# Ten of the gather windows move into the second layer: five destination blocks of layer 1 are summed from gathered rows instead of from streamed blocks

## The chip, the cores and the metric

The kernel runs on one core of one Trainium2 chip. The metric is the device time of one execution in microseconds (us). Three executions of the kernel before took 1515.6, 1515.96 and 1516.13 us; their median is 1515.96 us.

## The reference: a three-layer mean-aggregating graph network

There are 6,250 nodes with 128 features and 206,250 directed edges (100,000 random pairs in both directions and one loop for each node), sorted by destination. What is computed, cut to its core:

```python
def _mean_agg(x, src, dst, n):
    msg_sum = jax.ops.segment_sum(x[src], dst, num_segments=n)
    cnt = jax.ops.segment_sum(jnp.ones((src.shape[0], 1), x.dtype), dst, num_segments=n)
    return msg_sum / jnp.maximum(cnt, 1.0)
def _sage_conv(x, src, dst, Wl, bl, Wr):
    return _mean_agg(x, src, dst, x.shape[0]) @ Wl.T + bl + x @ Wr.T

h = jnp.maximum(_layernorm(x), 0.0)
h = relu(batch_norm(sage_conv(h, ..., Wl0, bl0, Wr0)))   # 128 -> 256 features
h = relu(batch_norm(sage_conv(h, ..., Wl1, bl1, Wr1)))   # 256 -> 256
h = sage_conv(h, ..., Wl2, bl2, Wr2)                     # 256 -> 128
out = x + log_softmax(h)
```

## The kernel before

The 6,250 destination nodes are cut into 25 blocks of 250 (`BD`), the source nodes into 49 tiles of 128 (`NA`). The segment sum is done as a dense product. In layer 0 the kernel builds, for each destination block, a matrix of edge counts (49 tiles of 128 x 250, f16, 3 MB in all), uses it at once and stores it in DRAM as `c_blocks`. Layers 1 and 2 load these blocks back into `ring`, which has two slots, and multiply them with the features. The features are kept in f16 as a high and a low part (`parts`, seen as `wide` in layer 1 with 256 features and as `small` in layer 2 with 128).

**Sweeps.** In layers 1 and 2 the blocks are visited in a fixed order (`orders`). Two blocks that lie in the two slots are swept together (`sweeps`, lines 158 to 162): one matmul of 500 columns serves both. A layer-1 pair sweep has 49 tiles x 2 parts (high, low) x 2 halves of the features = 196 such matmuls. What is left over is swept alone with matmuls of 250 columns. In layer 1, 25 blocks make 12 pair sweeps and one single sweep. Sweep 0 of a layer is special: TensorE also transposes the normalized features (`pe_pair`), ScalarE rounds them to the high part (`act_hi`) and VectorE subtracts to get the low part (`dve_lo`), 25 pairs of tiles in turn. A count called a step runs through the later sweeps (`places`, line 170): one step is two matmuls of 500 columns in a pair sweep, or four of 250 in a single one, and there are 49 of them for each block.

**The rest of a block.** After a sweep VectorE scales the sums to means (`dve_means`), and TensorE computes the two linear products of the block, 16 f32 matmuls in layer 1 (`pe_product1`, L1165 and L1168). They are put into the next sweep at given steps (`dense_lin`, line 179): at step `NA // 4` = 12 and 49 steps later.

**Gathered blocks.** Some blocks (`loose`) are not swept. Their features come row by row from a table in DRAM: `table_store` writes the f16 features there (high and low part side by side, 512 B a row in layer 2, 1024 B in layer 1), and GpSimd fetches 128 rows with one indirect DMA (`pool_round`). TensorE adds them up with a one-hot matrix (`pe_round`, L1193): the 125 nodes of half a block, a window, lie in four groups of 31 or 32 nodes, and a round takes one tile of 128 edges for each of them, so it has 4 indirect DMAs and 4 matmuls whose outputs go to 32 partitions each; the ninth and last round of a window has 5. Three rounds' buffers (`NGOT`) let GpSimd run ahead; a later round first waits for `t_round`, that TensorE has used the buffer. The steps at which TensorE takes the rounds are spread evenly over the layer (`at`, line 198). After a window TensorE transposes its sums (`pe_group_turn`), and ScalarE scales them (`act_gmean`). Before the change the gathered blocks are 21 and 22, and only in layer 2: 4 windows, 36 rounds, 148 DMAs. Layer 1 gathers nothing.

**Queues.** All order is written out by hand, one stream for each engine. SyncE issues the block loads (`block_load`, L1552: quarters of a block, each when the quarter of the slot has been used), GpSimd the indirect DMAs.

## Time and profile before

| | |
|---|---|
| median of three executions | 1515.96 us |
| the profiled execution | 1516.13 us, of it 1514.4 us span |
| TensorE busy | 1408.8 us (93%) |
| VectorE, ScalarE, GpSimd busy | 545.7, 531.9 and 282.5 us |
| mean granted TensorE clock | 0.987 |

The span runs from the first to the last instruction. A granted clock of 1.00 is 2.4 GHz. The stages follow one another: layer 0 to about 560 us, sweep 0 of layer 1 to 621 us, the rest of layer 1 to 1187 us, layer 2 to the end. In a timeline row the first number is the start, the second the time from the first start to the last end of a run of equal instructions; a run's matmuls overlap, so what one costs is the distance of two starts divided by their number.

### The profile page before, as it was taken

How to read it: one execution, taken by the hardware profiler on the slowest of the kernel's cores; microseconds unless marked ns; L12 is line 12 of the kernel's file. 1: busy time of each engine (PE TensorE's matmuls, PEld its weight loads, DVE VectorE, ACT ScalarE, POOL GpSimd, SP SyncE). 2: the span in 40 equal slices, each digit the busy share in tenths (PEclk: the TensorE clock that was granted, in tenths of full speed). 3: DMA queues.
4: the chain of work that ended last, by engine and by line, in shares of the span. 5: the costliest groups of instructions: out<-in, count | busy, mean ns of one | idle time of the engine just before them, and what ended most of it. 6: DMA issues, size and time to landing. Idle time of an engine off the chain costs nothing.

```text
span 1514.4 us, 31217 instructions
## 1 busy us (share of the span) xinstructions
PE 1408.8 (93%) x13761; PEld 873.5 (58%) x13761; DVE 545.7 (36%) x1001; ACT 531.9 (35%) x866; POOL 282.5 (19%) x266
## 2 busy tenths in 40 slices
PE   1399999999999999999999999999999899999996
PEld 1377777777767775554545545454557764444444
DVE  6968777777778753100000000000001212222123
ACT  4887878787877847200000000000000420000001
POOL 3422131313040200000000000000000024666640
PEclk9999999999999999999999999999999999999998
DMA  5244444544444442333443333434321487888882
GB/s 161 91 186 155 160 168 189 189 181 181 175 162 175 176 154 82 133 132 127 140 161 132 133 122 133 142 132 157 130 92 47 126 308 269 316 313 308 315 303 80
DMA packets 73812, 258.78 MB, mean 171 GB/s; under 512 B 12544, under 2 KB 42296, under 8 KB 70456
## 3 DMA queue, kind: packets, MB, share of 16 engines
q1 hardware_dynamic: 62860, 238.64, 44.3%
q0 software_dynamic: 7600, 16.45, 3.6%
q8 instruction: 112, 1.84, 0.5%
q10 hardware_dynamic: 3212, 1.63, 0.4%
q14 instruction: 28, 0.23, 0.0%
HBM read 171.85 MB, written 84.83 MB: 169 GB/s over the span
## 4 chain that ended last, share of the span: by engine, by line
PE 84%; ACT 7%; DVE 2%; issue 2%; another core or an unknown queue 2%; DMA 1%; POOL 0%; ACTq 0%; DVEq 0%; SPq 0%
PE bank L1568 30%; PE cells L1568 16%; PE bank L1150 15%; PE cells L1142 7%; PE bank L1165 4%; PE bank L1168 4%; ACT ring L653 3%; PE bank L1571 2%; ACT junk L601 2%; PE bank L1910 1%; PE cells L1649 1%; DMA parts<-in_pairs_dram,last_i 1%; PE cells L1193 1%; PE cells L1638 0%
## 5 line engine op out<-in xcount | busy, mean ns | idle before, releaser
L1568 PE MATMUL bank<-ring,parts 128*128 128x500 f16 x2254 | 501.6, 375 | 0.6 <-DVE parts L1623 0.4
L653 ACT CAST ring<-cells 128x980 f16<-128x980 f32 (+1 forms) x325 | 335.4, 1057 | 109.6 <-PE cells L1142 96.5
L1568 PEld LDWEIGHTS bank<-ring,parts 128*128 128x128 f16 x2254 | 214.2, 96 | 246.4 <-issue 7.1
L1150 PE MATMUL bank<-ring,parts 128*128 128x250 f16 (+1 forms) x2450 | 319.7, 272 | 2.7 <-ACT ring L653 2.3
L517 POOL DMA_INDIRECT hots<-table,src_i x148 | 140.3, 948 | 792.7 <-DMA table<-parts 708.6
L1568 PE MATMUL cells<-ring,parts 128*128 128x500 f16 x1176 | 251.3, 372 | 0.0
L881 DVE TENSOR_TENSOR hots<-iotas,tab 128x980 f16<-128x980 f16 (+3 forms) x262 | 245.6, 996 | 11.3 <-ACT tab L617 11.3
L1150 PEld LDWEIGHTS bank<-ring,parts 128*128 128x128 f16 (+1 forms) x2450 | 216.3, 98 | 35.2 <-ACT ring L653 3.7
L1695 ACT ACTIVATE Z<-bank,vec 128x250 f32<-128x250 f32 x48 | 19.9, 465 | 530.2 <-PE bank L1168 530.2
L1568 PEld LDWEIGHTS cells<-ring,parts 128*128 128x128 f16 x1176 | 112.5, 96 | 134.8
L961 DVE BATCH_NORM_STATS2 st<-Z 128x6 f32<-128x250 f32 x96 | 35.5, 412 | 394.5 <-ACT Z L1695 361.6
L1142 PE MATMUL cells<-hots 64*128 64x49 f16 x4670 | 107.2, 186 | 43.7 <-DVE hots L881 34.8
L1142 PEld LDWEIGHTS cells<-hots 64*128 64x128 f16 x4670 | 80.4, 95 | 96.9 <-issue 51.5
L1822 ACT ACTIVATE junk<-rows_i 128x128 f32<-128x128 f32 (+1 forms) x49 | 14.7, 301 | 231.1 <-DVE rows_i L1874 160.9
L881 DVE TENSOR_TENSOR parts<-iotas,tab 128x2560 f16<-128x2560 f16 (+1 forms) x88 | 83.0, 984 | 1.2 <-ACT tab L617 1.2
L1168 PE MATMUL bank<-agm,wl 128*128 128x250 f32 x288 | 76.5, 374 | 0.0
L1165 PE MATMUL bank<-Z,wr 128*128 128x250 f32 x288 | 76.4, 374 | 0.0
L469 POOL DMA_INDIRECT rows_i<-in_dst_rows_dram,row_i x25 | 36.3, 1451 | 198.1 <-DVE row_i L746 192.3
L1168 PEld LDWEIGHTS bank<-agm,wl 128*128 128x128 f32 x288 | 54.8, 190 | 6.0
L1165 PEld LDWEIGHTS bank<-Z,wr 128*128 128x128 f32 x288 | 52.4, 189 | 7.5
L1601 ACT ACTIVATE Z<-Z,bnw 128x256 f32<-128x256 f32 (+2 forms) x76 | 45.9, 655 | 1.8 <-DVE bnw L1590 1.6
L1142 PE MATMUL cells<-parts 64*128 64x49 f16 x1580 | 35.7, 186 | 11.1 <-ACT ring L653 8.5
(198 smaller groups left out, 771.5 us busy)
## 6 DMA issues: line engine op xcount, KB each, us to landing
ring<-c_blocks SPq DMA_DIRECT2D x132, 750.0 KB
c_blocks<-ring SPq DMA_DIRECT2D x25, 3062.5 KB
ring<-c_blocks SPq DMA_DIRECT2D x44, 812.5 KB
rcb<-rc_row SPq DMA_DIRECT2D x73, 125.0 KB
Z<-in_x_dram SPq DMA_DIRECT2D x4, 768.0 KB, 7.2
out_dram<-rows_i SPq DMA_DIRECT2D x24, 128.0 KB
hots<-table,src_i POOLq DMA_INDIRECT x148
table<-parts SPq DMA_DIRECT2D x2, 768.0 KB
```

The source lines that it names most:

```text
L469: pool.indirect_dma_start(out=rows_i[:, k, :], out_offset=None, in_=dst_rows, in_offset=bass.IndirectOffsetOnAxis(ap=row_i[:, c:c + 1], ax ...
L517: pool.indirect_dma_start(out=got[layer][:, 5 * (r % NGOT) + i, :], out_offset=None, in_=tables[layer], in_offset=bass.IndirectOffsetOnAxi ...
L601: act.activation(junk[:, 0:R], smp_i[:, :], ACT.Sign, bias=thr_h[:, c:c + 1], scale=-1.0, accum_out=s1[:, c:c + 1]).then_inc(a_sample, 1)
L653: act.copy(blk[c % 2][:, :, :].rearrange("p a (d g) -> p a d g", d=GD)[:, :, :, GPS * i:GPS * i + n], cells[t % 2][:, :, 0:n * NA].rearran ...
L881: ins = dve.tensor_tensor(o[:, 0:q, :, :], iota2[:, 0:w, :].unsqueeze(1).to_broadcast((P, q, w, 2)), place.unsqueeze(2).to_broadcast((P, q ...
L961: dve.bn_stats(st[:, m, b, :], Z[:, m, BD * b:BD * b + BD]).then_inc(v_stats, 1)
L1142: ins = pe.matmul(cells[t % 2][:, h, NA * g:NA * g + NA], bs[HE * h:HE * h + HE, q0 + g // 2, :, g % 2], ps[HE * h:HE * h + HE, q0 + g // ...
L1150: return pe.matmul(bank[b][:, 0:BD], view[0:r, a, part, m * P:m * P + P], blk[s][0:r, a, :], start=(a, part) == (0, 0), stop=(a, part) == ...
L1165: pe.matmul(bank[b][:, BD * m:BD * m + BD], wr[layer][:, k, m * P:m * P + P], Z[:, k, BD * c:BD * c + BD], start=(k == 0), stop=False)
L1168: ins = pe.matmul(bank[b][:, BD * m:BD * m + BD], wl[layer][:, k, m * P:m * P + P], mean[:, k, :], start=False, stop=(k == nk - 1))
L1568: ins = pe.matmul(bank[b][:, 0:2 * BD].rearrange("p (s d) -> p s d", s=2), lhs, ring[0:r, :, BD * a:BD * a + BD], start=(a, part) == (0, 0 ...
L1601: act.activation(Z[:, k, c0:c0 + w], Z[:, k, c0:c0 + w], ACT.Relu, bias=bnw[:, layer, 5, k:k + 1], scale=bnw[:, layer, 4, k:k + 1]).then_i ...
```

## The change

`NGB` (2 gathered blocks) becomes `NG1` = 5 for layer 1 and `NG2` = 2 for layer 2. The loose blocks are now 18 to 22: layer 1 gathers all five, layer 2 blocks 18 and 19. Layer 1 then visits 20 blocks, which make 10 sweeps in the layer's loop after sweep 0: 8 pair sweeps and 2 single ones (before 11 pair sweeps and 1 single). SyncE and ScalarE write the layer-1 table during sweep 0. The layer-1 products move from step 12 to step 6 of a sweep. The tables of windows grow from 16 to 40 rows, and the total of the loose counts is summed from two parts.

```diff
--- before.py
+++ after.py
@@ -24,7 +24,8 @@
 NHOT = 4
 NBT = 4
 NTAB = 8
-NGB = 2
+NG1 = 5
+NG2 = 2
 WIN = 31
 WT = (9, 9, 9, 10)
 WE = 1280
@@ -54,7 +55,7 @@
     NB = N // BD
     NT = -(-E // P)
     FULL = NA - 1
-    assert N % BD == 0 and GPS * NA <= 512 and NT * P <= EP and NB >= NGB + 4
+    assert N % BD == 0 and GPS * NA <= 512 and NT * P <= EP and NB >= NG1 + 4
     flat_pairs = pairs.rearrange("r c two -> (r c) two")
     pe, dve, act, pool, sp = nc.tensor, nc.vector, nc.scalar, nc.gpsimd, nc.sync
 
@@ -115,8 +116,8 @@
         return NST * (h // NHB) + min(NST, SPH * (h % NHB) + SPH) - 1
 
 
-    loose = list(range(NB - 2 - NGB, NB - 2))
-    gathered = [[], [], loose]
+    loose = list(range(NB - 2 - NG1, NB - 2))
+    gathered = [[], loose, loose[0:NG2]]
     W = 8 * len(loose)
     wins = [[2 * loose.index(b) + h for b in gathered[layer] for h in range(2)] for layer in range(3)]
     gbase = [0, 0, len(wins[1])]
@@ -177,7 +178,7 @@
 
 
     dense_lin = [{}, {}, {}]
-    for layer, a0 in ((1, NA // 4), (2, NA // 4)):
+    for layer, a0 in ((1, NA // 8), (2, NA // 4)):
         o = orders[layer]
         for u, js in enumerate(sweeps[layer][1:]):
             for k, j in enumerate(sweeps[layer][u]):
@@ -1090,9 +1091,15 @@
                                           ALU.add).then_inc(v_own, 1)
                         own.up()
                         parts_at = [batches[q][0] + 1 for q in range(len(batches)) if loose_part(q)]
-                        assert len(parts_at) == 1
                         dve.tensor_scalar(tot[:, NB + 1:NB + 2], tot[:, parts_at[0]:parts_at[0] + 1], -1.0, None,
-                                          ALU.mult).then_inc(v_tot, 1)
+                                          ALU.mult).then_inc(v_own, 1)
+                        dve.wait_ge(v_own, own.up())
+                        for k in parts_at[1:-1]:
+                            dve.tensor_tensor(tot[:, NB + 1:NB + 2], tot[:, NB + 1:NB + 2], tot[:, k:k + 1],
+                                              ALU.subtract).then_inc(v_own, 1)
+                            dve.wait_ge(v_own, own.up())
+                        dve.tensor_tensor(tot[:, NB + 1:NB + 2], tot[:, NB + 1:NB + 2],
+                                          tot[:, parts_at[-1]:parts_at[-1] + 1], ALU.subtract).then_inc(v_tot, 1)
                         dve_norms(own)
                     elif c == NB and i == 7:
                         dve_spread(own)
@@ -1663,6 +1670,9 @@
             v = vbase[1]
             rcb_load(v)
             rcb_load(v + 1)
+            for k in range(2):
+                table_here(sp, a_hi1, v_lo1, 2, xcuts[k + 1])
+                table_store(sp, 1, wide, xcuts[k], xcuts[k + 1])
             for u in range(1, len(sweeps[1])):
                 for k in range(4):
                     for j in sweeps[1][u]:
@@ -1688,6 +1698,11 @@
                     act_normalize(0, 2, t + 2, a_relu1)
                 if t + 1 < npair:
                     act_hi(wide, 2, 256, t + 1, t_pair, a_hi1)
+                if t == (xcuts[3] - 1) // 2 + 2:
+                    table_here(act, a_hi1, v_lo1, 2, xcuts[3])
+                    table_store(act, 1, wide, xcuts[2], xcuts[3])
+            table_here(act, a_hi1, v_lo1, 2, NA)
+            table_store(act, 1, wide, xcuts[3], NA)
             for t in range(NA * (D1 - 2)):
                 for b in products(1, t - 2):
                     act.wait_ge(t_lin, lin_no(1, b))
```

TensorE at the start of layer 1's sweep 1, as written before (L1568 is the sweep, L1165 and L1168 the product):

```order
L1568 MATMUL bank<-ring,parts 128x500 x12
L1568 MATMUL cells<-ring,parts 128x500 x26
L1165 MATMUL bank<-Z,wr 128x250 x2
L1168 MATMUL bank<-agm,wl 128x250 x2
L1165 MATMUL bank<-Z,wr 128x250 x2
L1168 MATMUL bank<-agm,wl 128x250 x2
L1568 MATMUL cells<-ring,parts 128x500 x98
```

The same place now (L1575 is the sweep, L1172 and L1175 the product, L1200 a gather round, whose outputs are 32 partitions x 512 columns):

```order
L1575 MATMUL cells<-ring,parts 128x500 x14
L1172 MATMUL bank<-Z,wr 128x250 x2
L1175 MATMUL bank<-agm,wl 128x250 x2
L1172 MATMUL bank<-Z,wr 128x250 x2
L1175 MATMUL bank<-agm,wl 128x250 x2
L1575 MATMUL cells<-ring,parts 128x500 x62
L1200 MATMUL cells<-hots,tab 32x512 x4
L1575 MATMUL cells<-ring,parts 128x500 x22
L1200 MATMUL cells<-hots,tab 32x512 x4
```

The product stands 12 matmuls earlier (6 steps), and from step 37 on a round stands after every 20 to 22 sweep matmuls, fewer where a product lies between.

GpSimd in layers 1 and 2, before:

```order
L1966 COMPARE_AND_BRANCH
L517 DMA hots<-table,src_i 128x256 x148
L1966 UNCONDITIONAL_BRANCH
```

and now:

```order
L1981 COMPARE_AND_BRANCH
L518 DMA hots<-table,src_i 128x512 x370
L518 DMA hots<-table,src_i 128x256 x148
L1981 UNCONDITIONAL_BRANCH
```

370 indirect DMAs of 128 rows x 512 numbers (1024 B) have come in ahead of the 148 of layer 2.

## Rows read from the trace of the kernel before

**Rows 1.** The page: TensorE's busy line, the chain by engine, two DMA queues

```profile
PE 1408.8 (93%) x13761; PEld 873.5 (58%) x13761; DVE 545.7 (36%) x1001; ACT 531.9 (35%) x866; POOL 282.5 (19%) x266
PE 84%; ACT 7%; DVE 2%; issue 2%; another core or an unknown queue 2%; DMA 1%; POOL 0%; ACTq 0%; DVEq 0%; SPq 0%
...
q1 hardware_dynamic: 62860, 238.64, 44.3%
q0 software_dynamic: 7600, 16.45, 3.6%
```

**Rows 2.** Busy time by stage (stretch: length, busy us of each engine, clock, DMA)

```profile
core 0: us, PE busy (x) PEld busy (x) DVE busy (x) ACT busy (x) POOL busy (x), PEclk, DMA share, GB/s
...
621.05:1150.67 529.62, 529.62 (x2511) 272.95 (x2509) 34.28 (x88) 18.23 (x44) 0.00 (x0) 1.00 0.39 132
...
1232.60:1514.40 281.80, 262.26 (x1379) 130.94 (x1377) 62.34 (x159) 25.41 (x132) 140.28 (x148) 0.96 0.79 276
```

**Rows 3.** Timeline of TensorE, one pair sweep of layer 1 with its two products

```profile
677.91 20.86 PE L1568 MATMUL bank<-ring,parts 128*128 128x500 f16 x98
698.60 1.00 PE L1165 MATMUL bank<-Z,wr 128*128 128x250 f32 x4
...
701.98 15.37 PE L1568 MATMUL bank<-ring,parts 128*128 128x500 f16 x72
717.19 1.01 PE L1568 MATMUL cells<-ring,parts 128*128 128x500 f16 x4
```

**Rows 4.** Timeline of TensorE, the single sweep and layer 1's end

```profile
1167.97 10.43 PE L1571 MATMUL bank<-ring,parts 128*128 128x250 f16 x96
1178.24 1.01 PE L1212 MATMUL bank<-Z,wr 128*128 128x250 f32 x4
```

**Rows 5.** Timeline of TensorE, two gather rounds and a turn in layer 2

```profile
1412.14 0.29 PE L1193 MATMUL cells<-hots,tab 128*32 128x256 f16 x4
1412.37 3.13 PE L1568 MATMUL bank<-ring,parts 106*128 106x500 f16 x14
...
1417.75 0.40 PE L1193 MATMUL cells<-hots,tab 128*32 128x256 f16 x5
1418.09 3.76 PE L1568 MATMUL bank<-ring,parts 128*128 128x500 f16 x17
...
1423.81 0.27 PE L1202 MATMUL cells<-cf,gsum 128*128 128x128 f32 x1
1424.01 0.29 PE L1193 MATMUL cells<-hots 128*32 128x256 f16 x4
```

**Rows 6.** Timeline, last table stores and first gathers of layer 2 (512 B rows)

```profile
1231.16 1.43 ACTq L458 DMA_DIRECT2D table<-parts  x2
1232.59 1.57 SPq L1552 DMA_DIRECT2D ring<-c_blocks  x2
1237.22 1.06 POOL L517 DMA_INDIRECT hots<-table,src_i  x1 [708.65 <-DMA table<-parts]
...
1238.59 0.96 POOL L517 DMA_INDIRECT hots<-table,src_i  x1 [0.30 <-issue]
1239.86 0.95 POOL L517 DMA_INDIRECT hots<-table,src_i  x1 [0.30 <-issue]
```

**Rows 7.** Timeline of GpSimd, indirect DMAs of 1024 B rows in layer 0

```profile
16.10 0.94 POOL L469 DMA_INDIRECT rows_i<-in_dst_rows_dram,row_i  x1 [0.30 <-issue]
17.35 0.94 POOL L469 DMA_INDIRECT rows_i<-in_dst_rows_dram,row_i  x1 [0.30 <-issue]
...
90.40 2.00 POOL L469 DMA_INDIRECT rows_i<-in_dst_rows_dram,row_i  x1 [15.37 <-DVE row_i L746]
```

**Rows 8.** The line L469, all 25: from issue to landing

```profile
DMA to landing us min/median/max: 2.7/3.5/6.1
```

**Rows 9.** Groups of GpSimd by line: mean ns of one

```profile
L517 POOL DMA_INDIRECT hots<-table,src_i x148 | 140.3, 948 | 792.7 <-DMA table<-parts 708.6 <-issue 42.2 <-remote 23.5
L469 POOL DMA_INDIRECT rows_i<-in_dst_rows_dram,row_i x25 | 36.3, 1451 | 198.1 <-DVE row_i L746 192.3 <-issue 5.8
```

**Rows 10.** Timeline, the end of sweep 0 of layer 1

```profile
618.96 0.42 DVE L1623 TENSOR_TENSOR parts<-cells,parts 106x256 f16<-106x256 f32 x1 [1.00 <-ACT parts L1617]
...
621.09 1.64 DVE L890 SCALAR_TENSOR_TENSOR agm<-bank,bnw,rcb 128x250 f32<-128x250 f32 x4 [1.71 <-PE bank L1568]
```

**Rows 11.** Timeline of SyncE's queue around the start of layer 1

```profile
545.97 4.81 SPq L450 DMA_DIRECT2D rcg<-rc_row  x4
560.62 0.82 SPq L407 DMA_DIRECT2D rcb<-rc_row  x2
582.17 40.20 SPq L1552 DMA_DIRECT2D ring<-c_blocks  x8
```

**Rows 12.** Timeline of TensorE, layer 2, after a wait

```profile
1258.55 0.40 PE L1193 MATMUL cells<-hots,tab 128*32 128x256 f16 x4 [3.17 <-DVE tab L1009]
1258.88 5.18 PE L1568 MATMUL bank<-ring,parts 128*128 128x500 f16 x12
1263.85 1.32 PE L1910 MATMUL bank<-Z,wr 128*128 128x250 f32 x4
```

## Prediction, made before the changed kernel ran

> **What bounds the kernel now.** I read the page first. TensorE is busy 1408.8 of 1514.4 us, and 84% of the chain that ended last lies on it [rows 1]. Then the table by stage: between 621.05 and 1150.67 us, layer 1 after its first sweep, TensorE is busy for the whole 529.62 us at a granted clock of 1.00, GpSimd does nothing, VectorE 34 us, ScalarE 18 us, and the DMA engines are used to 0.39 [rows 2]. So there TensorE alone sets the pace, and one us less of matmuls is one us less of time, as long as nothing that is added becomes slower than TensorE. Last I read the timeline of one sweep, for what a matmul costs from start to start: 98 matmuls of 500 columns take 698.60 - 677.91 = 20.69 us, 0.211 each; a product takes 701.98 - 698.60 = 3.38 us [rows 3]; a matmul of 250 columns (1178.24 - 1167.97) / 96 = 0.107 us [rows 4].
>
> **What goes from TensorE.** Three pair sweeps fewer: 3 x 196 x 0.211 = 124.1 us. One single sweep more: 196 x 0.107 = 21.0 us. Net -103.1 us. The 25 products stay 25; those of the gathered blocks only move.
>
> **What comes to TensorE.** Ten windows of nine rounds: 80 rounds of 4 matmuls and 10 of 5. Layer 2 shows the operation with 256 columns: the next sweep matmul starts 0.23 us after a round of 4 and 0.34 us after one of 5 [rows 5]. Four matmuls one after the other would take 4 x 0.107 = 0.43 us, so the four run side by side, and only the fifth, which goes to the same 32 outputs as the fourth, adds a stream of 0.11. With 512 columns a stream is 0.213 us (0.211 x 512 / 500 is 0.216; both read off the same row). From below: only the stream doubles, a round of 4 costs 0.23 + 0.107 = 0.34, one of 5 0.34 + 2 x 0.107 = 0.55, together 80 x 0.34 + 10 x 0.55 = 32.7 us. From above: everything doubles, 0.46 and 0.68, together 43.6 us. Ten turns of two transposes: one costs 0.20 with what surrounds it [rows 5], I take 0.3, 3 us. TensorE's own sum is -103.1 + 32.7 + 3 = -67.4 us, or -56.5 by the upper price.
>
> The excess of a round over its stream, 0.12 us, could be a fixed price or grow with the columns. The Trainium skill (TensorEngine Tiling (Array Packing), Key Properties) says that going to another tiling mode drains the engine, which here happens twice a round and does not depend on the columns. By that rule the lower price holds (-67.4); by plain scaling the upper one does. The trace agrees that there is an excess, 0.23 against a stream of 0.107, and has only one width, so it can't say which.
>
> **GpSimd, the new second bound.** 80 x 4 + 10 x 5 = 370 indirect DMAs come into layer 1, where GpSimd has been idle. One takes 0.95 us and the next starts 0.30 us later: a pitch of 1.25 us, in layer 2 with 512 B rows [rows 6] and in a quiet piece of layer 0 with 1024 B rows [rows 7] (17.35 - 16.10). So the size of a row doesn't matter, and GpSimd needs 370 x 1.25 = 462 us. When can it start? The last piece of the table is ready when VectorE ends the last low part at 618.96 + 0.42 = 619.4 [rows 10]. In layer 2 GpSimd started 1237.22 - 1231.16 = 6.1 us after the last stores were issued, of half as many bytes and with a block load beside them [rows 6]; for twice the bytes I take 6 to 10, so GpSimd starts at 626 to 630. TensorE reaches the first round at step 37: 621.05 + 37 x 0.422 + 3.38 = 640.1. By then the first round's 4 DMAs are issued (635 at the latest) and, with 2.5 to 3.5 us to land [rows 8], there.
>
> From the first round on both walk at nearly the same pace. TensorE: round 89 stands at step 840, so 803 steps x 0.422 = 338.9, 18 products of swept blocks and 4 of gathered ones 22 x 3.38 = 74.4, rounds 32 (43 by the upper price), turns 3: 448 us (459). GpSimd: three rounds are fetched ahead, the other 87 have 358 DMAs x 1.25 = 447.5 us, and the last needs 2.5 us more to land: 450. By the lower price GpSimd is late by about 2 us, and since the rounds with 5 DMAs (6.25 us) meet a TensorE pace of 448 / 89 = 5.0 us with about 7 us of lead, I take 5 us of waits of TensorE for rows; by the upper price none. So the two bounds give -62.4 and -56.5. I take the middle, -60: 1516.1 - 60 = 1456 us. The profiled execution (1516.13, with 1.7 us outside its span) stands 0.2 us above the median.
>
> **What costs nothing, and its cover.** (a) Five 3 MB blocks fewer are loaded, but the DMA share was 0.39 and loads were issued three quarters of a sweep ahead: no gain. (b) The gathers bring 370 x 131 KB = 48.5 MB. Queue 0 moved 16.45 MB in 3.6% of 1514 us, 302 GB/s when it had the engines [rows 1]: 161 us over 470, which raises the DMA share from 0.39 to about 0.73. Layer 2 ran at 0.79 [rows 2] and TensorE was busy 262 of 282 us there, so this cover is thin; it is a rival below. (c) SyncE's two table stores stand ahead of the first block loads. The first load moves from 582.17 [rows 11] to when half of the low parts exist, about 592; that data is needed at 621, and 3 MB with a store beside it need about 10 us at 300 GB/s. Covered by 18 us. (d) ScalarE issues three stores (0.4 and 1.43 us, [rows 6]) in sweep 0, where it waits for TensorE in every turn: under 1 us. (e) The product at step 6 begins 2.5 us after the sweep; the means it needs end at 621.09 + 1.64 = 622.7 [rows 10], TensorE is there at 623.6. (f) The count columns `rcg` are 2.5 times as many short pieces: 4.81 us of issue become some 12, from 545.97 to 558, before SyncE's next work at 560.62 [rows 11]. (g) VectorE's one more subtraction, two wider casts, ten one-hots and twenty foldings lie on an engine that is busy for 34 of 530 us. (h) Layer 2 keeps 36 rounds and 148 DMAs, for other blocks.
>
> **Rivals.** *Rows that come late.* GpSimd's pitch or the landing is what TensorE waits for, because 1024 B gathers share the DMA engines with block loads. With a lead of about 7 us and equal paces, each 0.05 us on the pitch is 370 x 0.05 = 18 us. For it: share 0.73, landings up to 6.1 us [rows 8], and a wait of 3.17 us in layer 2 was followed by 12 matmuls at 0.41 us each, granted clock 0.50 or 1.2 GHz, 2.5 us more [rows 12]. Against it: in layer 2, at a higher share, the mean DMA took 948 ns [rows 9]. At a pitch of 1.30 the time is 1474, at 1.35 it is 1492.
>
> *GpSimd held up (slower).* The 25 indirect DMAs of layer 0 took 1451 ns on the mean [rows 9], the first of a batch 2.00 us [rows 7], while VectorE was at work. At 1.45 + 0.30 = 1.75 us a DMA, GpSimd needs 370 x 0.5 = 185 us more and sets the time: 1456 + 185 - 4 = 1637 us. It decides from a pitch of 1.25 + 60 / 370 = 1.41 us on: above that the kernel is slower than before. Against it: VectorE is busy for 6% of layer 1 and in layer 2, at 22%, the mean was 948 ns [rows 2, 9]. The Trainium skill (SBUF — State Buffer, Who interferes with whom) says that an operation of VectorE in a mode that uses both ports locks GpSimd out for its whole length. By that rule copies from SBUF count, and VectorE's work in layer 1 reads nearly always PSUM, so the slow case would not come; the trace agrees, with slow DMAs in layer 0 only.
>
> *Column groups one after the other.* If 512-column rounds did not overlap, 370 x 0.213 = 79 us instead of 33: TensorE's sum is -21, 1495 us. Against it stand the 0.23 us [rows 5].
>
> *It doesn't do what it says.* The layers after layer 0 run only if all edges fit their windows, else the general path does, many times slower. A group of 31 nodes has 1023 edges on the mean and room for 1152, four standard deviations (32); 40 such groups make this very unlikely.
>
> **Chances.** The forecast (both paces as read, 1449 to 1464) 0.62; late rows (1464 to 1500) 0.28; serial rounds 0.03; GpSimd held up 0.05; the general path or another loss 0.02. The range reaches from TensorE's lower sum alone, 1449, less 1, to a pitch of 1.31, 1478. What three executions can tell from no change is about 0.2%, 3 us. Faster 0.93, no change 0.01, slower 0.06.
>
> **What the profile after would show.** A sweep period of pair sweeps of 48.15 us plus about 9 rounds at 0.34 to 0.46; layer 1 from 621 to about 1118 instead of 1178; 370 entries of GpSimd at 1.25 us with almost no gap; an idle GpSimd between rounds means TensorE sets the pace, waits of TensorE ahead of the gather line mean that GpSimd does. Sweep 0 is to end at 621 +- 1 and layer 2 to take 282 us as before. Wrong: indirect DMAs over 1.0 us, waits for quarters of a block, granted clock below 1.00 in layer 1, rounds of 0.8 us.

## The result, and the profile after

The changed kernel took 1542.41 us (1541.72 to 1542.49, four runs), the kernel before on the same chip 1515.78 us: ratio 1.0182, 95% interval 1.0163 to 1.0201. It was slower by 26.6 us where the prediction said faster by 60. On another chip the same file later took 0.9648 of before (interval 0.9623 to 0.9672), faster by 51.5 us. Both results have to be explained, and the second is the easier one, so both profiles stand here side by side. "The 1515 us kind" is a chip on which the kernel before takes 1514.7 to 1515.8 us (the first one and those numbered 3 and 1), "the 1497 us kind" one on which it takes 1496.5 to 1496.7 us (5, 13 and 0).

The page of the changed kernel on the first chip (busy line, chain by engine, two queues), to be read against [rows 1]:

```profile
PE 1377.2 (90%) x13759; PEld 845.9 (55%) x13759; DVE 558.5 (36%) x1023; ACT 540.8 (35%) x906; POOL 638.5 (42%) x636
PE 70%; another core or an unknown queue 9%; ACT 7%; issue 6%; POOL 4%; DVE 3%; DMA 1%; DVEq 0%; ACTq 0%; SPq 0%
...
q1 hardware_dynamic: 63132, 225.47, 41.2%
q0 software_dynamic: 25408, 65.24, 13.8%
```

The same lines of the same kernel on chip 13:

```profile
PE 1341.1 (93%) x13759; PEld 837.4 (58%) x13759; DVE 558.1 (39%) x1023; ACT 543.0 (38%) x906; POOL 642.9 (45%) x636
PE 79%; ACT 6%; POOL 4%; DMA 4%; issue 3%; DVE 3%; ACTq 0%; DVEq 0%; SPq 0%
```

The work is the same; the first chain has 9% on "another core or an unknown queue", in a kernel that has one core, and 6% on "issue" (the engine waited for nothing that the profile shows). The place is layer 1. From the first means to the last product (first start of the line below to that of the line after it) the kernel before needed 1178.24 - 621.09 = 557.15 us [rows 4, 10]. The changed kernel on the first chip, timelines of VectorE and TensorE:

```profile
620.66 1.63 DVE L891 SCALAR_TENSOR_TENSOR agm<-bank,bnw,rcb 128x250 f32<-128x250 f32 x4 [1.71 <-PE bank L1575]
...
1200.77 1.01 PE L1219 MATMUL bank<-Z,wr 128*128 128x250 f32 x4
```

and on chip 13:

```profile
610.74 1.63 DVE L891 SCALAR_TENSOR_TENSOR agm<-bank,bnw,rcb 128x250 f32<-128x250 f32 x4 [1.71 <-PE bank L1575]
...
1117.82 1.01 PE L1219 MATMUL bank<-Z,wr 128*128 128x250 f32 x4
```

580.1 us against 507.1 us. GpSimd's rows of 621 to 1100 us say how it differs; first chip, then chip 13:

```profile
L518 POOL DMA_INDIRECT hots<-table,src_i x320 | 304.6, 952 | 265.5 <-DMA table<-parts 104.9 <-issue 90.2 <-remote 55.3
```

```profile
L518 POOL DMA_INDIRECT hots<-table,src_i x370 | 352.9, 954 | 219.2 <-issue 108.8 <-DMA table<-parts 104.3 <-PE cells L1200 6.1
```

A DMA costs 0.95 us on both, as in [rows 9]. But on the first chip 55.3 us went into waits that end "remote", and on chip 13 none. The profile writes "remote" when no instruction that raises the awaited semaphore ended shortly (1.5 us) before the raise was recorded; with one core at work that means a release recorded late. What such a wait is shows in the timeline of all engines (without weight loads) on the first chip, at the end of sweep 1:

```profile
745.39 0.60 PE L1575 MATMUL bank<-ring,parts 106*128 106x500 f16 x2
745.83 3.12 PE L1575 MATMUL cells<-ring,parts 128*128 128x500 f16 x14
746.30 0.95 POOL L518 DMA_INDIRECT hots<-table,src_i  x1 [0.30 <-issue]
747.55 0.95 POOL L518 DMA_INDIRECT hots<-table,src_i  x1 [0.31 <-issue]
751.16 0.80 SPq L1559 DMA_DIRECT2D ring<-c_blocks  x2
751.17 1.63 DVE L891 SCALAR_TENSOR_TENSOR agm<-bank,bnw,rcb 128x250 f32<-128x250 f32 x4 [22.26 <-remote]
751.36 0.94 POOL L518 DMA_INDIRECT hots<-table,src_i  x1 [2.87 <-remote]
...
752.18 2.00 PE L1172 MATMUL bank<-Z,wr 128*128 128x250 f32 x4 [3.24 <-DVE agm L891]
```

The sweep's last matmuls run at 745.39 to 746. SyncE (its next quarter) and VectorE (the means) wait for just that, and start at 751.16 and 751.17, some 5 us late. GpSimd had stopped at 748.50 and started in the same moment, 751.36. Until 748.50 it had issued one DMA after another. TensorE then waits 3.24 us for the means. SyncE and GpSimd start again together at 673.02 and 673.34 too. TensorE stumbles too, with waits for nothing that the profile shows (its timeline, first chip; idle time before a row in brackets):

```profile
652.52 0.37 PE L1175 MATMUL bank<-agm,wl 128*128 128x250 f32 x1
653.58 0.37 PE L1175 MATMUL bank<-agm,wl 128*128 128x250 f32 x1 [0.68 <-issue]
654.29 0.47 PE L1175 MATMUL bank<-agm,wl 128*128 128x250 f32 x1 [0.34 <-issue]
654.98 0.37 PE L1175 MATMUL bank<-agm,wl 128*128 128x250 f32 x1 [0.22 <-issue]
...
656.72 3.73 PE L1575 MATMUL cells<-ring,parts 128*128 128x500 f16 x10
660.39 0.40 PE L1200 MATMUL cells<-hots,tab 128*32 128x512 f16 x4
```

Four matmuls start 0.7 to 1.06 us apart instead of 0.21, and the next ten of 500 columns take (660.39 - 656.72) / 10 = 0.37 us each against 0.211 before; as after the wait in [rows 12], most of them run at 1.2 GHz, 0.41 us each. Busy time over 621 to 1100 us, the changed kernel on the first chip and on chip 13 (columns as in [rows 2]):

```profile
621.00:1100.00 479.00, 436.77 (x2103) 207.70 (x2100) 40.58 (x95) 22.90 (x70) 304.57 (x320) 0.96 0.58 192
```

```profile
621.00:1100.00 479.00, 471.50 (x2536) 243.82 (x2534) 46.07 (x107) 26.25 (x80) 352.94 (x370) 1.00 0.63 211
```

From the first means to the last product TensorE stood idle for about 50 us in 26 places on the first chip, 7 us in 4 places on chip 13 (the 5.2 us at the layer's end, which both have, not counted). The clock, 0.96 against 1.00 over some 529 us of matmuls, costs about 19 us more (an estimate from these two numbers). These make 62 of the 73 us; the other 11 are not accounted for. (The profiled execution of the first chip took 1533.44 us, 9 us less than its four others, so these stretches understate the loss.)

### The profile page after: what moved, and what is told of

The parts are those of the page before. It is cut to its first block, busy times and chain, and to the rows that moved or that the text cites. A ratio compares the mean times of both kernels' runs of the same rounds, so it can differ in the third digit from the quotient of the medians.

```text
span 1531.7 us, 31641 instructions
## 1 busy us (share of the span) xinstructions
PE 1377.2 (90%) x13759; PEld 845.9 (55%) x13759; DVE 558.5 (36%) x1023; ACT 540.8 (35%) x906; POOL 638.5 (42%) x636
## 4 chain that ended last, share of the span: by engine, by line
PE 70%; another core or an unknown queue 9%; ACT 7%; issue 6%; POOL 4%; DVE 3%; DMA 1%; DVEq 0%; ACTq 0%; SPq 0%
PE bank L1575 24%; PE bank L1157 14%; PE cells L1575 7%; PE cells L1149 7%; POOL hots L518 4%; PE bank L1172 3%; PE bank L1175 3%; ACT ring L654 3%; PE cells L1200 2%; PE bank L1578 2%; ACT junk L602 2%; PE cells L1578 2%; PE bank L1925 1%; PE cells L1656 1%
## 5 line engine op out<-in xcount | busy, mean ns | idle before, releaser
L518 POOL DMA_INDIRECT hots<-table,src_i x518 | 491.8, 949 | 458.8 <-DMA table<-parts 191.5
L1575 PE MATMUL bank<-ring,parts 128*128 128x500 f16 x2058 | 475.4, 379 | 11.6 <-issue 11.0
L1575 PEld LDWEIGHTS bank<-ring,parts 128*128 128x128 f16 x2058 | 193.0, 97 | 245.8 <-issue 43.4
L1575 PE MATMUL cells<-ring,parts 128*128 128x500 f16 (+1 forms) x784 | 179.0, 378 | 9.8 <-issue 9.7
L1575 PEld LDWEIGHTS cells<-ring,parts 128*128 128x128 f16 (+1 forms) x784 | 72.7, 97 | 104.4 <-issue 27.2
L1172 PE MATMUL bank<-Z,wr 128*128 128x250 f32 x288 | 78.6, 382 | 7.3 <-issue 4.0
L1175 PE MATMUL bank<-agm,wl 128*128 128x250 f32 x248 | 68.4, 381 | 1.2 <-issue 1.2
L1172 PEld LDWEIGHTS bank<-Z,wr 128*128 128x128 f32 x288 | 53.7, 195 | 16.2 <-issue 9.2
L481 POOL DMA_INDIRECT parts<-in_pairs_dram,first_i x25 | 29.0, 1162 | 73.2 <-DVE first_i L754 67.7
L1175 PEld LDWEIGHTS bank<-agm,wl 128*128 128x128 f32 x248 | 48.2, 195 | 7.2 <-issue 1.6
```

The lines of the kernel that those rows point to most:

```text
L518: pool.indirect_dma_start(out=got[layer][:, 5 * (r % NGOT) + i, :], out_offset=None, in_=tables[layer], in_offset=bass.IndirectOffsetOnAxi ...
L1172: pe.matmul(bank[b][:, BD * m:BD * m + BD], wr[layer][:, k, m * P:m * P + P], Z[:, k, BD * c:BD * c + BD], start=(k == 0), stop=False)
L1175: ins = pe.matmul(bank[b][:, BD * m:BD * m + BD], wl[layer][:, k, m * P:m * P + P], mean[:, k, :], start=False, stop=(k == nk - 1))
L1575: ins = pe.matmul(bank[b][:, 0:2 * BD].rearrange("p (s d) -> p s d", s=2), lhs, ring[0:r, :, BD * a:BD * a + BD], start=(a, part) == (0, 0 ...
```

## The experiments

All ratios are to the kernel before in the same job on the same chip.

| run | kind of chip | us | ratio and interval |
|---|---|---|---|
| e2 half the DMAs | 1497 | 1438.76 | 0.9612 [0.9596, 0.9628] |
| e3 half-width rows | 1497 | 1442.03 | 0.9634 [0.9618, 0.9650] |
| e4 four blocks | 1497 | 1449.49 | 0.9685 [0.9669, 0.9701] |
| e5 the changed kernel | 1497 | 1445.12 | 0.9648 [0.9623, 0.9672] |
| e6 thin block loads | 1497 | 1440.12 | 0.9623 [0.9601, 0.9644] |
| e7 one matmul a round | 1497 | 1443.92 | 0.9651 [0.9629, 0.9672] |
| e8 four blocks | 1497 | 1450.85 | 0.9698 [0.9676, 0.9721] |
| e9 before (one run) | 1515 | 1509.65 | |
| e10 products at step 12 | 1515 | 1545.85 | 1.0206 [1.0184, 1.0227] |
| e11 half the DMAs | 1515 | 1455.35 | 0.9605 [0.9587, 0.9623] |
| e12 half-width rows | 1515 | 1542.28 | 1.0177 [1.0154, 1.0200] |
| e13 thin block loads | 1515 | 1539.12 | 1.0165 [1.0146, 1.0184] |
| e14 four blocks | 1515 | 1473.02 | 0.9730 [0.9708, 0.9752] |
| e15 and a fifth DMA | 1515 | 1530.56 | 1.0109 [1.0083, 1.0135] |
| e16 and a filler | 1515 | 1467.82 | 0.9695 [0.9672, 0.9718] |
| e17 five blocks, short break | 1497 | 1473.39 | 0.9844 [0.9827, 0.9860] |
| e18 break each second round | 1497 | 1459.57 | 0.9753 [0.9736, 0.9769] |
| e19 four blocks, short break | 1497 | 1450.73 | 0.9696 [0.9680, 0.9712] |

A variant that issues none of the 370 DMAs of layer 1 (e1) gave no time, so no run shows the changed kernel's TensorE work with an idle GpSimd. The edits below are cut to the lines that matter.

**Three variants that seemed to cure it.** The first theories were A (the releases of other engines come late while GpSimd issues indirect DMAs back to back), B (bytes crowd the DMA engines) and C (the rounds' matmuls are dear).

```diff
 e2: -            for i, (tile, j) in enumerate(tiles_of(t)):      # in pool_round
     +            for i, (tile, j) in dmas_of(layer, t):           # layer 1: i even only
 e3: -  out=got[layer][:, 5 * (r % NGOT) + i, :],        in_=tables[layer],
     +  out=got[layer][:, 5 * (r % NGOT) + i, 0:256],    in_=  # layer 1: its table as rows of 512 B
 e4: -NG1 = 5
     +NG1 = 4
```

> The changed kernel with every second indirect DMA of layer 1 left out (190 of 370; 2 of 4, 3 of 5 in a round), all matmuls kept; half of the gathered rows are left out of the computation. Half the bytes and half the DMAs; GpSimd now pauses in every round. Theory A (late signals while GpSimd issues without a break) expects nearly all of the loss gone: 1450 to 1465 us. Theory B (bytes) expects about half of the 93 us between 1542 and 1449 left: about 1495 us. Theory C expects no change, 1540 us.

> The changed kernel with rows of 512 B instead of 1024 B in the 370 indirect DMAs of layer 1: the same number of DMAs at the same places, half the bytes; half of each gathered row is left out of the computation. Theory A expects no change, since GpSimd issues as many DMAs in a row: 1530 to 1545 us. Theory B (bytes) expects half of the loss gone, about 1495 us. Theory C expects 1540 us.

> The changed kernel with NG1 = 4: layer 1 gathers four blocks, 19 to 22, in 296 indirect DMAs, and sweeps 21 blocks, so that one single sweep is left instead of two. TensorE's own sum: two pair sweeps fewer than before (-82.8), 64 rounds of 4 and 8 of 5 (+26 to +35), 8 turns (+2.4): -54 to -45, 1462 to 1471 us. GpSimd needs 370 of the 500 us left and pauses in every round. Theory A expects 1462 to 1480 us. Theories B and C expect four fifths of the 93 us loss on top: about 1535 us.

All three reached 0.961 to 0.969 with 6 to 11 us of idle TensorE, 5.2 of them at the layer's end. In e3 GpSimd issued 328 DMAs without a pause and nothing came late, so I took A for refuted. That was a false conclusion: the kernel before took 1496.7 us in that job, 19 us less than on the first chip, and the changed kernel itself had not run there.

**The control.**

> The changed kernel as it is, beside the kernel before on the same chip, as a control for the variants that ran on another chip. Theory B (the bytes of 1024 B gathers and the block loads crowd the DMA engines, releases and rows come late in spells, TensorE idles and then runs at half clock) expects a ratio near the first one, 1.01 to 1.03, with some 50 us of idle time of TensorE in layer 1. Rival D (the loss belonged to the chip of the first run) expects 0.96 to 0.98 and under 15 us of idle time.

0.9648: rival D was right, the loss shows only on one kind of chip. So e2 to e4 say nothing about the cause. They are still useful as what the variants cost where nothing comes late.

**Two prices, on the 1497 us kind.**

```diff
 e6: -            sp.dma_start(blk[...][:, a0:a1, :], C_dram[c, :, BD * a0:BD * a1]
     +            rows = 32 if layer == 1 else P
     +            sp.dma_start(blk[...][0:rows, a0:a1, :], C_dram[c, 0:rows, BD * a0:BD * a1]
 e7: -            for i, (tile, j) in enumerate(tiles_of(t)):      # in pe_round
     +            for i, (tile, j) in list(enumerate(tiles_of(t)))[0 if layer == 2 else -1:]:
```

> The block loads of layer 1 bring only partitions 0 to 31, a quarter of the bytes (about 47 of 63 MB less); all 370 indirect DMAs with 1024 B rows stay, and so does everything on TensorE. The sums of layer 1 are then made of stale counts. Theory B expects the idle time of TensorE in layer 1 to fall to under 12 us and the ratio to before to about 0.96. Rival E (the gathers alone are too many for their own queue, whatever the loads do) expects the idle time as in the changed kernel, 40 us and more.

> All DMAs stay; TensorE does only the last matmul of each of the 90 rounds of layer 1 (280 of 370 left out, so the sums of the gathered blocks are not whole). Theory C (the rounds' matmuls are what is dear) expects 50 us and more below the changed kernel. Theory B expects that TensorE's work falls by 80 x 0.13 to 0.25 and 10 x 0.45 us, 15 to 25 us, and that the idle spells stay, so 5 to 25 us below the changed kernel.

e6: idle time of TensorE in layer 1 fell from 7.0 to 1.8 us, the time by 5 us, hardly clear of the noise (the intervals of e5 and e6 touch). Shared DMA engines cost no more than that here. e7: 1.2 us less, which is no difference that four runs can tell, where I had expected 5 to 25. Timeline of TensorE in e5 (rounds of four matmuls), then in e7 (rounds of one):

```profile
647.04 4.82 PE L1575 MATMUL cells<-ring,parts 128*128 128x500 f16 x22
651.80 0.40 PE L1200 MATMUL cells<-hots,tab 128*32 128x512 f16 x4
652.13 4.82 PE L1575 MATMUL cells<-ring,parts 128*128 128x500 f16 x22
658.44 0.40 PE L1200 MATMUL cells<-hots,tab 128*32 128x512 f16 x4 [1.50 <-DMA hots<-table,src_i]
```

```profile
646.16 4.82 PE L1575 MATMUL cells<-ring,parts 128*128 128x500 f16 x22
650.92 0.39 PE L1200 MATMUL cells<-hots,tab 128*32 128x512 f16 x1
651.24 3.98 PE L1575 MATMUL cells<-ring,parts 128*128 128x500 f16 x18
```

A period of 22 sweep matmuls and a round is 652.13 - 647.04 = 5.09 us with four matmuls and 651.24 - 646.16 = 5.08 with one. Less 22 x 0.211, a round costs 0.45 and 0.44 us. Three of the four matmuls cost nothing, they run side by side with the fourth; what costs is the stream of the one, 0.21, and going there and back, 0.24. Theory C falls for this kind; for the other kind it falls with e11 below, which does all 370 matmuls and has no loss.

**Which part of the change, and is it the whole chip that is slower?** e9 is the kernel before; e10 sets `NA // 8` back to `NA // 4` in `dense_lin`.

> The kernel before, unchanged, for its trace on another chip than the one where it took 1516 us. If the slowness of the first chip sits where gathers and block loads run together (theory F: on that chip releases through semaphores come late while GpSimd's indirect DMAs run; on the others not), layer 1 of this kernel, which has no gathers, takes the same here (621 to 1178 us) and the 19 us less than 1516 are found in layer 2: no waits named remote or another core there, GpSimd's pauses in step with TensorE. If the first chip was slower in everything (rival G: a lower clock or slower memory throughout), the stages are shorter here in proportion, layer 0 and layer 1 too.

> One part of the change is undone: the products of layer 1 stay at step 12 of a sweep and 49 steps later; everything else is as in the changed kernel. Theory: the place of the products costs and gives nothing by itself, only the rounds' places move with them; within 3 us of the changed kernel where it reaches 1445 us, with the same 6 to 9 us of waits of TensorE for gathered rows. Rival H: the move to step 6 is itself a cost (the product waits for the means); then this kernel is 5 us or more faster.

This job ran on a chip of the 1515 us kind, so e9 gave a second trace of before there: layer 1 took 1176.24 - 619.10 = 557.14 us, as in the first, and GpSimd's waits in layer 2 again had 24.6 us "remote" (23.5 in [rows 9]). A trace of before on the 1497 us kind was not taken. What can be compared is the changed kernel: it reaches the first means at 610.74 there and at 620.66 on the first chip, so 9.9 of the 19 us lie ahead of layer 1's gathers. Sweep 0, in which GpSimd issues nothing, begins at 558.19 and 567.56 and takes 52.6 and 53.1 us: 9.4 of the 9.9 us are from layer 0, and there GpSimd issues indirect DMAs, in batches of four for the rows, the first and the last edges. The traces show where. GpSimd's waits for VectorE after two of these batches, first chip, then chip 13:

```profile
190.72 2.02 POOL L481 DMA_INDIRECT parts<-in_pairs_dram,first_i  x1 [11.37 <-DVE first_i L754]
198.87 1.99 POOL L491 DMA_INDIRECT parts<-in_pairs_dram,last_i  x1 [2.38 <-DVE last_i L764]
```

```profile
188.65 2.02 POOL L481 DMA_INDIRECT parts<-in_pairs_dram,first_i  x1 [11.07 <-DVE first_i L754]
196.26 1.99 POOL L491 DMA_INDIRECT parts<-in_pairs_dram,last_i  x1 [1.84 <-DVE last_i L764]
```

These waits are 0.3 and 0.5 us longer on the first chip, and it falls further behind chip 13 with each set of batches: by 0.1 us at 90.69, 1.8 at 172.17, 3.2 at 253.64. Between 133 and 172 us, where GpSimd issues none, it doesn't fall behind at all. Layer 2 of the changed kernel, with 148 more, takes 330.9 against 325.8 us. So, as far as these traces show, the two kinds differ where indirect DMAs run, and layers 0 and 2 of the kernel before have them too. Against G stands this, and that the rates are equal (granted clock 1.00, 0.211 us a matmul, 0.95 us a DMA). e10: 1.0206, no better than the changed kernel's 1.0182; the products' place is not the cause (rival H falls), and the loss came back on a second chip.

**Bytes or DMAs.** e2, e3 and e6 again, now on a chip of the 1515 us kind.

> Every second indirect DMA of layer 1 left out (180 of 370; the sums of the gathered blocks are not whole), now hoping for a chip on which the kernel before takes about 1515 us and the changed one about 1543. There all engines' releases come about 2.7 us late once in 14 DMAs of GpSimd. Theory K (the stalls go by the number of indirect DMAs) expects half as many stalls, TensorE idle in layer 1 about 25 to 30 us instead of 55 to 64. Theory B (by bytes over the DMA engines) expects fewer than a third, under 15 us. If before takes 1497 us here, the chip doesn't show the stalls, and the run says nothing new beside its ratio of 0.96.

> All 370 indirect DMAs, each row 512 B instead of 1024 B (the sums are not whole). On a chip of the 1515 us kind: theory K expects as many stalls as in the changed kernel, some 26 to 30, with 45 us and more of idle time of TensorE in layer 1 and a ratio of 1.00 to 1.02; theory B expects a fall to under 25 us and a ratio of 0.97 to 0.985. On a chip of the 1497 us kind 0.963 as before.

> All 370 indirect DMAs of 1024 B rows, block loads of layer 1 with a quarter of their bytes (the sums are made of stale counts). On a chip of the 1515 us kind: theory K expects 45 us and more of idle time as in the changed kernel, ratio 1.00 to 1.02; theory B expects under 20 us and 0.965 to 0.98. On a chip of the 1497 us kind 0.962 as before.

Half the gathers' bytes: 1.0177. A quarter of the loads' bytes: 1.0165. Busy time and DMA share of e13 from 621 to 1100 us:

```profile
621.00:1100.00 479.00, 432.12 (x2074) 208.94 (x2072) 41.14 (x95) 22.79 (x70) 304.38 (x320) 0.95 0.44 119
```

At 0.44 of the DMA engines and 119 GB/s TensorE is as badly off as at 0.58 and 192 GB/s, so theory B is refuted. Half the DMAs took the loss away wholly: 0.9605, with one wait of 1.0 us in layer 1 besides its end. Theory K (stalls by the number of DMAs) had asked for half as many stalls, so K as written is refuted too. In e11 GpSimd has two DMAs a round and waits for TensorE after nearly each: its chain never gets long. Theory A, which I had dropped, foretells that.

**The chain broken, closed and broken otherwise.** With four blocks a round of GpSimd takes 5.0 of some 6.6 us.

```diff
 e14: NG1 = 4
 e15: NG1 = 4, and in dmas_of, which pool_round and landed use:
      +        l = list(tiles_of(t))
      +        return l + l[0:1] if layer == 1 and len(l) == 4 else l
 e16: NG1 = 4, and in pool_round after the DMAs:
      +            if layer == 1:
      +                pool.wait_ge(p_pad, r + 1)
      +                pool.tensor_scalar(pad[:, :], ones[:, :], 0.0, -1024.0, ALU.is_equal, ALU.mult).then_inc(p_pad, 1)
```

> NG1 = 4 (complete): 296 indirect DMAs, GpSimd has 1.66 us of slack in each round, so it waits for TensorE at each round and breaks its chain. On a chip of the 1515 us kind: theory A (releases of the other engines come late as long as GpSimd issues indirect DMAs without a break, and GpSimd then doesn't see that it may pause) expects few stalls, since the chain breaks each round or each second one as in layer 2: TensorE idle in layer 1 under 20 us, ratio 0.97 to 0.98. Theory K' (a stall for each 14 DMAs as long as they come in rounds of four) expects 20 stalls, 40 us idle, ratio near 1.00.

> As e14 with a fifth indirect DMA in each of the 64 rounds of four, whose rows nobody uses: 360 DMAs, 6.25 of some 6.66 us of a round, 0.4 us of slack. Outputs as in e14. Theory A expects the stalls back (the chain hardly breaks): on a chip of the 1515 us kind 40 us and more of idle time of TensorE in layer 1, ratio 1.00 to 1.02; on a chip of the 1497 us kind within 1% of e14 of that kind.

> As e14 with one ordinary GpSimd instruction (128x128 f32 tensor_scalar, about 1.2 us) after the DMAs of each round of layer 1, which fills most of its slack; 296 DMAs. If the chain of indirect DMAs is what matters (theory A), the break between two rounds of DMAs stays 1.5 us and stalls stay as few as in e14, within 0.5% of it. If any unbroken activity of GpSimd does it (rival L), or if it is only the missing slack of the slower rows, this one goes like e15.

GpSimd from 621 to 1100 us in e14 and in e15:

```profile
L518 POOL DMA_INDIRECT hots<-table,src_i x296 | 281.5, 951 | 286.9 <-DMA table<-parts 104.1 <-PE cells L1200 89.8 <-issue 76.7
```

```profile
L523 POOL DMA_INDIRECT hots<-table,src_i x316 | 301.5, 954 | 269.5 <-DMA table<-parts 103.9 <-issue 87.1 <-remote 61.5
```

With slack GpSimd's waits have a name, the round that TensorE has just used: 89.8 us, and "remote" is down to 16.3. One more DMA a round, which nobody reads, and 61.5 us are "remote", TensorE's matmuls are the same, its idle time in layer 1 goes from 4 to 41 us, and the kernel from 0.973 to 1.011. In e16 part of the same slack is filled by an ordinary instruction instead; GpSimd's timeline:

```profile
709.85 0.65 POOL L525 TENSOR_SCALAR pad<-ones 128x128 f32<-128x128 f32 x1
710.77 1.01 POOL L520 DMA_INDIRECT hots<-table,src_i  x1 [0.27 <-issue]
712.08 0.95 POOL L520 DMA_INDIRECT hots<-table,src_i  x1 [0.30 <-issue]
713.34 0.96 POOL L520 DMA_INDIRECT hots<-table,src_i  x1 [0.31 <-issue]
714.61 0.96 POOL L520 DMA_INDIRECT hots<-table,src_i  x1 [0.30 <-issue]
715.63 0.64 POOL L525 TENSOR_SCALAR pad<-ones 128x128 f32<-128x128 f32 x1
```

and of e15, a stretch of the same place:

```profile
715.62 0.95 POOL L523 DMA_INDIRECT hots<-table,src_i  x1 [0.30 <-issue]
716.88 0.95 POOL L523 DMA_INDIRECT hots<-table,src_i  x1 [0.31 <-issue]
720.66 0.95 POOL L523 DMA_INDIRECT hots<-table,src_i  x1 [2.83 <-remote]
```

e16 is at 0.9695, its four runs (1466.5 to 1468.9) all below e14's (1472.9 to 1473.3). The filler was 0.65 us, not the 1.2 that I had written; with it a round took 5.8 us, three quarters of a us more than its DMAs, and TensorE lost nothing. That speaks against rival L (any unbroken activity), but doesn't rule it out: GpSimd still waited 39.0 us for TensorE in e16, against 16.9 in e15, so the slack was not filled as far.

The traces also hold a direct measure. They record raises of semaphores with their times (not all of them on the 1515 us kind). Here are the raises by TensorE's rounds from 630 to 1110 us (layer 2: 1240 to 1430), each set against the end of the last round matmul that raises before it, and how many of them came over 0.5 us after it:

| stretch | kind | recorded raises | late |
|---|---|---|---|
| changed kernel, layer 1 | 1497 (e5) | 89 | 0 |
| changed kernel, layer 1 | 1515 | 65 | 45 |
| e12, half-width rows | 1515 | 67 | 44 |
| e13, thin block loads | 1515 | 69 | 42 |
| e15, a fifth DMA | 1515 | 56 | 34 |
| e14, four blocks | 1515 | 61 | 14 |
| e16, filler | 1515 | 62 | 10 |
| e11, half the DMAs | 1515 | 85 | 0 |
| before, layer 2 | 1515 | 23 | 13 |

On the 1497 kind the raise is recorded within 0.03 us. So it is the release that is late, not only the engine that waits for it. In layer 1 of the kernel before, without indirect DMAs, none of TensorE's 59 raises is late on the 1515 kind either. The number of DMAs per us alone doesn't order the table: layer 2 of before issues one each 1.52 us on the mean, mostly eight or nine in a row, and e14 one each 1.57, mostly four in a row. Theory A is what is left, that long rows of indirect DMAs without a break hold the releases back. One thing it is not cleared of: a late release itself keeps GpSimd from pausing where it could, so that long rows are in part what follows. A break in the changed kernel with its 370 DMAs would tell.

**A break in the changed kernel itself.** As e16, but with an instruction of 128x1, and five blocks.

```diff
 e17: +                pool.tensor_scalar(pad[:, :], ones[:, 0:1], 0.0, ...)    # each round
 e18: +            if layer == 1 and r % 2 == 0:                                # each second round
 e19: as e17, NG1 = 4
```

> The changed kernel (five blocks, 370 DMAs, complete) with one very short ordinary GpSimd instruction (128x1, about 0.1 us, with a wait for its forerunner) after the DMAs of each round of layer 1. Theory A (the unbroken chain of indirect DMAs holds back the others' releases): the stalls go, and what is left is GpSimd's slower pace, 90 rounds x 0.35 us = 32 us less about 2 of cover: on a chip of the 1515 us kind ratio 0.97 to 0.985, TensorE waiting for rows in short pieces; on one of the 1497 us kind 0.98 to 0.99. Rival M (a break must be a microsecond and more to let the releases through): the ratio stays at 1.01 to 1.03 on a chip of the 1515 us kind.

> The same with the short instruction after each second round. Theory A, if a chain of 8 to 9 DMAs is short enough: 16 us less of GpSimd's pace than e17, ratio 0.965 to 0.98 on a chip of the 1515 us kind. Rival M: as the changed kernel, 1.01 to 1.03.

> Four blocks (complete) with the short instruction after each round: 296 DMAs, 5.35 of 6.66 us of a round. Theory A: as good as e16 or better, 0.967 to 0.970 on a chip of the 1515 us kind, since the chain breaks and the slack stays. Rival M: as e14, 0.973.

This job fell on the 1497 us kind, so whether the short break cures the changed kernel on the other kind was not seen and stays open. It gave the price: 1473.4 us each round, 1459.6 each second one, against 1445.1 without (another chip of this kind), 28 and 14 us for 90 and 45 breaks, 0.31 us each. With five blocks GpSimd has no slack, and each 0.3 us on it is paid in full (TensorE waits 28.3 us for rows in layer 1 of e17, against 7). With four blocks it costs nothing (1450.7 against 1450.9).

**The version to keep** is four blocks: 0.9685, 0.9698 (1497 us kind) and 0.9730 (1515 us kind). It beats before on the three chips on which it ran; the changed kernel is 0.4 to 0.5% faster than it on one kind and 4.6% slower on the other (there on different chips).

## Why the prediction was wrong, point by point

- *TensorE's own sum.* Right in kind, one term too small, and chip 13 shows it without the disturbance. I read a round's price only on its far side (0.23 us from its start to the next sweep matmul). The near side is a row of before that I passed over, just ahead of the second round of [rows 5]:

```profile
1416.18 1.64 PE L1568 MATMUL bank<-ring,parts 128*128 128x500 f16 x7
```

These 7 sweep matmuls take 1417.75 - 1416.18 = 1.57 us, 0.09 more than 7 x 0.211. With both sides a round of 512 columns is 0.45, not 0.34, and one of 5, with one stream of 0.21 more, about 0.66: 42.6 us instead of 32.7. The upper price of the prediction, 43.6, comes close by luck: it doubled everything, and the side that was left out made up for that. The excess over the stream is 0.33 - 0.107 = 0.22 at 256 columns and 0.45 - 0.213 = 0.24 at 512: a fixed price, not one that doubles. The rule of the Trainium skill (TensorEngine Tiling (Array Packing), Key Properties), that a change of tiling mode drains the engine, agrees.
- *Waits for rows.* Forecast 5 us, and 7.0 measured on chip 13 in four waits. The start of GpSimd was mis-sized: forecast for 626 to 630, it issued its first DMA at 633.11 on the first chip (623.13 on chip 13, where all lies 10 us earlier), and TensorE, there at 640, waited 1.56 us for the first round (1.77 on chip 13). The lead of 7 us did not exist at the start.
- *The sum on the 1497 us kind.* -103.1 + 42.6 + 3 + 7.0 = -50.5 us; layer 1 gave 507.1 - 557.15 = -50.1 (the second number is from the first chip; no trace of before on this kind exists), the whole kernel -51.5 against its own before. 0.9648 of 1515.96 is 1462.6 us, inside the range, 6.6 us above the forecast.
- *Covers (a) to (h).* The first means after sweep 0 began at 620.66 (forecast 621 +- 1) on the first chip. A DMA took 0.95 us at a pitch of 1.25 on every chip, and 13759 matmuls are recorded, as planned (13761 - 588 + 196 + 370 + 20).
- *The step that failed.* "From the first round on both walk at nearly the same pace": I took GpSimd's issue for free to everyone else as long as its own pitch held, and the pitch held. The term for what it does to the other engines' releases stood at nothing, without a reason. On the 1515 us kind, with 370 DMAs without slack, 45 of 65 recorded raises of TensorE's rounds are late, VectorE and SyncE start some 5 us late in the stretch shown, and GpSimd goes on only after 2 to 3 us of quiet, once in some 14 DMAs. The change had left GpSimd no slack (450 us of issue in 448 us of TensorE). Layer 1 cost 73 us more than on chip 13; e12 and e13 show that it isn't the bytes, e11, e14 and e15 that it comes and goes with the indirect DMAs and GpSimd's slack, and e16 that an ordinary instruction in part of the slack does no harm.
- *The rivals.* "Rows that come late" was priced by the pitch and came true with 7 us only on chip 13. "GpSimd held up" had the sign right, but neither the pitch nor the place. None of them had the loss on the engines that wait for each other. The sentence that argued with layer 2 (TensorE busy 262 of 282 us at a DMA share of 0.79) compared shares, but there GpSimd has slack in each round.
- *What I could have seen.* 23.5 us "remote" in [rows 9], 2% "another core or an unknown queue" in [rows 1], in a kernel with one core. Both were signs of it in layer 2 of before, and I priced them at nothing. That the same file is faster on other chips could not be read from one chip's trace, and 0.93 for faster was too sure.

**Open.** Why one kind of chip does this and the other doesn't, and by what path GpSimd's issue delays the others' releases; whether it is the length of the row without a break or the number of DMAs in a stretch; how short a break suffices; and whether the changed kernel with breaks would do on the 1515 us kind.

## What to carry to other kernels

Give GpSimd slack when it issues indirect DMAs in a long row: cut the number until it waits for its consumer in most rounds. Here 5.0 of 6.6 us a round was good and 6.25 was not; between them nothing was tried with indirect DMAs. A wait that ends "remote" on a single core is to be priced, also where it costs nothing yet. Before a variant on another chip is believed, run the unchanged case beside it: three "cures" here were only another chip.

## What the hardware showed that I had not expected

- Two kinds of chips under equal clocks and equal prices of single instructions: 1515 and 1497 us for one kernel, 1542 and 1445 us for another, 7% apart, and the two kernels change places.
- On one kind, releases between engines some 5 us late while GpSimd issues indirect DMAs without slack (296 with slack: 0.973; 360: 1.011 of before), and none late with half the DMAs. The 19 us between the kinds in the kernel before lie in layers 0 and 2, as far as the changed kernel's traces show, where its indirect DMAs are.
- TensorE fell to matmuls at 0.7 us starts with nothing to wait for, and then took 0.37 us for a matmul of 500 columns, most of them at 1.2 GHz.
- Four matmuls of a round, each to 32 partitions, cost as much as one (0.45 and 0.44 us), and going there and back costs 0.22 us at 256 columns and 0.24 at 512.
